# Two transformer layers on one Trainium2 core: PSUM banks by a plan of what is free first, the experts' weighted sums on GpSimd

## The chip, the cores and the metric

The program runs on one core of one Trainium2 chip. The metric is the device time of one execution in microseconds (us); the figure of a kernel is the median over its runs.

## The reference

Input x is 4 sequences of 1024 tokens of width 128, float32. Two layers follow, each of the form x + attention(norm(x)) + feed-forward(norm(x)), 16 heads of width 8.

```
layer 0: xn = layernorm(x)
         attention: q, k with rotary positions, softmax(q k^T / sqrt(8)) v, output matrix and bias (not causal)
         experts:   scores = xn @ gate_w + gate_b; the best 2 of 8 experts; softmax over the two scores
                    out = sum over the two: p_i * (relu(xn @ w1[e] + b1[e]) @ w2[e] + b2[e])
         x = x + attention + experts
layer 1: xn = layernorm(x)
         attention: causal, softmax(q k^T / sqrt(8)) v, output matrix
         ffn:       xq, w quantized blockwise (16) to FP4 and back; h = silu(xq @ wg) * (xq @ wu); quantized h @ wd
         x = x + attention + ffn
```

## The kernel before, in words

**Phases and slots.** A phase is one layer of one sequence (PHASES, eight of them, numbered 0 to 7: layer 0 of sequences 0 and 1, then layer 1 of sequence 0, and so on). The class Plan lays all work into 491 slots before the program is written. A slot holds one `step` (for four heads: scores with keys on the partitions, 128 keys by 512 queries, called E), one `quad` of a later set of rows (for four heads: scores with queries on the partitions, called M, of which only the row maxima are wanted), the `pv` product of the step before (into the PSUM tile pO), and side work: `xs` (PSUM-filling work such as projections, expert units `unit` and `y`, transposes), `small` (VectorE steps), `act`/`late` (ScalarE), `pool` (GpSimd) and `sp` (DMA issues). Each engine walks through the slots in order and executes its part; semaphores tie them.

**PSUM.** pO has one bank of its own. The other seven banks are the ring (RING = 7). Every E (one head), every M (one head) and every entry of `xs` takes one bank. TensorE writes E, `exps` on ScalarE (L854) reads it into PR; TensorE writes M, `maxima` on VectorE (L1201, and L1205 for masked tiles of layer 1) reduces it into mparts. In this kernel the n-th claim takes bank n mod 7, and before it `vacant` lets TensorE wait until the claim seven back has been read out (s_ex for E, s_mr for M, s_xA or s_xD for an entry of xs). TensorE executes in order: what waits holds up all that stands behind it.

```
r = plan.at[kind][k] - RING
if r >= 0:
    was, of = plan.ring[r]
```

**The experts' sum.** The tokens are scattered to rows in HBM ordered by expert (L784), 23 units of 128 rows go through the experts, and the results come back by indirect DMAs (`gather`, L800), eight tiles of 128x128 for the first expert (k = 0) into yg, which is the tile ra, and then eight for the second (k = 1). After each eight, VectorE's step `comb` adds them into the residual xr: 8 instructions of 128x128 (L1381), each xr = yg * weight + xr with the weight a number per partition, in four steps of two. So there are 4 sequences x 2 x 8 = 64 of them. The gathers of k = 1 wait on s_comb for the sums of k = 0, and the statistics of layer 1 (`stats`) come some slots behind the last sum. ra also serves as `sums` in the projections with rotary positions.

**GpSimd** has in its queue: the variance's power -1/2, the split of projections into bf16 parts (L759, L763, L767), scatters and gathers, and the rounding to FP4 (`round`, L811 to L831).

**VectorE and GpSimd lines** the text speaks of: L1268 normalises, L1381 is the experts' sum, L1439/L1440 split the row maxima for the tile msplit, L831 is a 128x512 product with an operand repeated along its blocks, L759 a 128x512 sum.

## Time and profile before

| what | value |
|---|---|
| median of 3 runs | 1598.43 us (1593.64 to 1598.57) |
| the profiled execution, its own time | 1606.22 us |
| its span | 1604.5 us |
| busy TensorE / VectorE / ScalarE / GpSimd | 91% / 83% / 70% / 36% of the span |
| mean granted TensorE clock | 0.956 of full speed |
| time per slot (491 slots) | 3.3 us |

PE in a row is TensorE, PEld its weight loads, DVE VectorE, ACT ScalarE, POOL GpSimd, SP SyncE, which issues most DMAs. A busy PE includes the modelled end of each matmul. "Lxxx" is a line of the kernel before.

### The profile page before, as it was taken

How to read it: one execution, taken by the hardware profiler on the slowest of the kernel's cores; microseconds unless marked ns; L12 is line 12 of the kernel's file. 1: busy time of each engine (PE TensorE's matmuls, PEld its weight loads, DVE VectorE, ACT ScalarE, POOL GpSimd, SP SyncE). 2: the span in 40 equal slices, each digit the busy share in tenths (PEclk: the TensorE clock that was granted, in tenths of full speed). 3: DMA queues.
4: the chain of work that ended last, by engine and by line, in shares of the span. 5: the costliest groups of instructions: out<-in, count | busy, mean ns of one | idle time of the engine just before them, and what ended most of it. 6: DMA issues, size and time to landing. Idle time of an engine off the chain costs nothing.

```text
span 1604.5 us, 34217 instructions
## 1 busy us (share of the span) xinstructions
PE 1459.2 (91%) x10557; PEld 583.9 (36%) x10557; DVE 1338.2 (83%) x3450; ACT 1129.7 (70%) x2580; POOL 578.4 (36%) x531
## 2 busy tenths in 40 slices
PE   3978989999999899989999999989999988989986
PEld 1112344443333544432333444333433432323332
DVE  6999877789887698999888789889878779978991
ACT  2267678788787467777878767768878845765675
POOL 3002302103253456440242263660152464554443
PEclk8599999999999899999999999999999977989998
DMA  6403273333271452221451135123372100600000
GB/s 172 102 8 100 73 184 110 106 87 91 88 183 52 120 116 83 59 82 36 134 120 51 37 113 134 49 82 99 111 165 82 39 26 2 152 9 15 2 2 14
DMA packets 169833, 131.84 MB, mean 82 GB/s; under 512 B 31597, under 2 KB 143158, under 8 KB 169654
## 3 DMA queue, kind: packets, MB, share of 16 engines
q1 hardware_dynamic: 165562, 121.26, 28.5%
q0 software_dynamic: 4096, 8.40, 1.7%
q8 instruction: 91, 1.49, 0.4%
q14 instruction: 84, 0.69, 0.1%
HBM read 88.50 MB, written 40.50 MB: 80 GB/s over the span
## 4 chain that ended last, share of the span: by engine, by line
PE 58%; DVE 26%; issue 6%; ACT 5%; POOL 3%; DMA 1%; SPq 0%; another core or an unknown queue 0%; DVEq 0%; ACTq 0%; POOLq 0%
PE ring L542 38%; PE pO L542 17%; DVE mparts L1201 15%; PE ring L545 3%; ACT PR L854 3%; DVE junk L1205 2%; DVE xr L1381 1%; DVE stats L1251 1%; ACT hid L925 1%; DVE hs L1493 1%; DVE xr L1501 1%; DVE am L1414 1%; DMA b1r<-in_b 1%; ACT parts L548 0%; DVE hs L1489 0%
## 5 line engine op out<-in xcount | busy, mean ns | idle before, releaser
L854 ACT ACTIVATE PR<-ring 128x512 f32<-128x512 f32 (+3 forms) x1792 | 882.4, 557 | 344.8 <-PE ring L542 333.7
L1201 DVE TENSOR_REDUCE mparts<-ring 128x1 f32<-128x512 f32 x1280 | 808.5, 682 | 84.4 <-PE ring L542 77.1
L542 PE MATMUL ring<-QX,KX 50*128 50x512 bf16 (+3 forms) x1792 | 543.7, 366 | 77.2 <-DVE mparts L1201 35.5
L542 PE MATMUL ring<-KX,QX 48*128 48x512 bf16 (+3 forms) x1792 | 556.8, 374 | 14.2 <-DMA QX<-scratch 14.1
L542 PE MATMUL pO<-PR,VX 128*18 128x512 f32 (+3 forms) x3584 | 444.0, 568 | 6.5 <-ACT PR L854 5.2
L542 PEld LDWEIGHTS ring<-QX,KX 50*128 50x128 bf16 x1792 | 127.5, 94 | 609.0 <-ACT PR L854 220.3
L1205 DVE CUSTOM_DVE_ANT_0 junk<-ring,diag 128x384 bf16<-128x384 f32 (+3 forms) x512 | 228.8, 486 | 46.0 <-PE ring L542 41.2
L811 POOL TENSOR_SCALAR bq<-bq 128x352 f32<-128x352 f32 (+1 forms) x40 | 47.2, 1179 | 349.7 <-ACT bq L964 349.3
L784 POOL DMA_INDIRECT rows_in<-xn,at x64 | 63.7, 996 | 228.8 <-PE pO L542 144.8
L542 PEld LDWEIGHTS ring<-KX,QX 48*128 48x128 bf16 x1792 | 127.3, 94 | 33.6 <-DVE mparts L1201 17.9
L925 ACT ACTIVATE hid<-ring,b1r 128x128 f32<-128x128 f32 x368 | 105.0, 369 | 27.7 <-PE ring L542 26.2
L542 PE MATMUL ring<-yx,w1r 128*128 128x128 f32 x736 | 107.8, 291 | 7.7 <-DMA b1r<-in_b 4.8
L542 PEld LDWEIGHTS pO<-PR,VX 128*18 128x18 f32 x3584 | 60.6, 96 | 132.0 <-issue 88.0
L800 POOL DMA_INDIRECT ra<-rows_out,at x64 | 61.6, 963 | 125.4 <-PE pO L542 89.2
L542 PEld LDWEIGHTS ring<-yx,w1r 128*128 128x128 f32 x736 | 91.7, 196 | 34.3 <-DVE mparts L1201 23.3
L542 PE MATMUL ring<-w2r,hid 128*128 128x128 f32 x736 | 97.5, 275 | 0.0
L542 PEld LDWEIGHTS ring<-w2r,hid 128*128 128x128 f32 x736 | 93.2, 197 | 0.9 <-issue 0.5
L767 POOL TENSOR_TENSOR parts<-rb,parts 128x512 bf16<-128x512 f32 x30 | 35.0, 1166 | 115.3 <-ACT parts L548 115.3
L542 PE MATMUL ring<-identb,laterb 128*128 128x128 bf16 x512 | 75.2, 230 | 0.0
L825 POOL TENSOR_SCALAR yq<-yq 128x352 f32<-128x352 f32 (+1 forms) x40 | 60.3, 1508 | 3.3
L820 POOL TENSOR_TENSOR bq<-hq,bq 128x352 f32<-128x352 f32 x64 | 59.7, 933 | 4.6
L548 ACT ACTIVATE yx<-ring 128x256 f32<-128x256 f32 (+1 forms) x96 | 36.0, 375 | 35.2 <-PE ring L542 33.8
(165 smaller groups left out, 1349.8 us busy)
## 6 DMA issues: line engine op xcount, KB each, us to landing
w1r<-in_w SPq DMA_DIRECT2D x92, 256.0 KB
w2r<-in_w SPq DMA_DIRECT2D x92, 256.0 KB
scratch<-parts SPq DMA_DIRECT2D x48, 256.0 KB, 3.3
scratch<-parts SPq DMA_DIRECT2D x96, 128.0 KB, 2.3
KX<-scratch SPq DMA_DIRECT2D x64, 192.0 KB, 4.4
QX<-scratch SPq DMA_DIRECT2D x128, 96.0 KB, 5.0
xg<-rows_in SPq DMA_DIRECT2D x92, 64.0 KB
rows_out<-yx SPq DMA_DIRECT2D x92, 64.0 KB
```

The costliest lines, as they stand in the source:

```text
L542: return nc.tensor.matmul(dst, lhsT, rhs, start=start, stop=stop, **kw)
L545: return nc.tensor.transpose(dst, src, ident[0:src.shape[0], 0:src.shape[0]])
L548: return nc.scalar.activation(dst, src, ACT.Copy)
L784: nc.gpsimd.indirect_dma_start(xs[b % 2], bass.IndirectOffsetOnAxis(at[b % 2][:, c:c + 1], 0), xn[0][:, c % T, :], None).then_inc(s_sc[b], 16)
L800: nc.gpsimd.indirect_dma_start(yg[:, D * t:D * t + D], None, ys[b % 2], bass.IndirectOffsetOnAxis(at[b % 2][:, c:c + 1], 0)).then_inc(s_yg ...
L811: ins = nc.gpsimd.tensor_scalar(b_, b_, 1.0, None, ALU.max)
L820: ins = nc.gpsimd.tensor_tensor(b_, dst, b_, ALU.subtract)
L825: ins = nc.gpsimd.tensor_scalar(y, y, SHIFT, SHIFT, ALU.add, ALU.subtract)
L854: nc.scalar.activation(PR[:, n % 2, HALF * j + off:HALF * j + HALF], ring[plan.bank("E", k)][:, off:HALF], ACT.Exp, scale=SCALE).then_inc( ...
L925: ins = nc.scalar.activation(hid[N % 2][:, P * fc:P * fc + P], src[:, P * fc:P * fc + P], ACT.Relu, bias=b1r[N % 2][:, fc:fc + 1])
L1201: v.tensor_reduce(dst, src[:, 0:w], axis=X, op=ALU.max).then_inc(s_mr, 1)
L1205: v.tensor_tensor_reduce(out=junk[k % 2][:, 0:w], in0=src[:, 0:w], in1=diag[:, HALF - w:HALF], scale=1.0, scalar=NEG, op0=ALU.add, op1=ALU ...
```

## The change

Two things change. First, Plan gets a method `banks`: it walks through all slots with a cost for each piece of work on TensorE, ScalarE and VectorE, keeps for each engine a clock in its own units, and gives each claim the bank that this account frees first. `vacant` then waits for whatever was last in that bank. Second, `comb` leaves VectorE's lists and goes to GpSimd's, with two halves of 512 columns instead of four steps of two tiles: a product of yg with the weights (128x512, weight repeated along a tile's columns) in place, then a sum into xr. GpSimd waits between the two on a new semaphore s_mul. s_comb now counts four per sequence, and VectorE waits on it before `stats` of layer 1, before `soft1`, and before each write of a projection (`pj`), since ra is shared. The steps after the sums of sequences 0 and 3 (phases 2 and 7: stats, projections, stores, loads) come one to three slots later.

```diff
@@ Plan
+    def banks(self):
+        work = {"P": [], "A": [], "D": []}
...
+        freeing = {"E": "ex", "M": "mx"}
+        time, at, clock, place = {}, [], {"P": 0, "A": 0, "D": 0}, {"P": 0, "A": 0, "D": 0}
+        held = [None] * RING
+        self.bank_of, self.was = {}, {}
+        def advance(who):
+            while place[who] < len(work[who]):
+                cost, needs, takes, gives = work[who][place[who]]
+                if any(t not in time for t in needs):
+                    return
+                clock[who] = max([clock[who]] + [time[t] + LAG for t in needs])
+                if takes is not None:
+                    free = lambda b: -1 if held[b] is None else time.get(held[b][1], math.inf)
+                    b = min(range(RING), key=free)
+                    clock[who] = max(clock[who], free(b) + LAG)
+                    self.bank_of[takes], self.was[takes] = b, held[b] and held[b][0]
...
     def bank(self, kind, k):
-        return self.at[kind][k] % RING
+        return self.bank_of[kind, k]
@@ tiles
-            i = self.chain("comb", i + T // 2 + 1, [("comb", p, k, h) for h in range(T // 2)], 2 if p in (1, 3) else 1)[-1] + 1
+            i += T // 2 + 1
+            for h in range(NH):
+                self.slot(i)["pool"].append(("comb", p, k, h))
+                i += 1
@@ gpsimd
-                                pool.wait_ge(s_comb, 2 * b + k)
+                                pool.wait_ge(s_comb, 4 * b + 2 * k)
...
+                        if e[0] == "comb":
+                            _, p, k, h = e
+                            b = PHASES[p][1]
+                            if h == 0:
+                                pool.wait_ge(s_yg[k], 16 * T * (b + 1))
+                                pool.wait_ge(s_xn, T * (p + 1))
+                            g_ = yg[:, HALF * h:HALF * h + HALF]
+                            g3 = g_.rearrange("p (t d) -> p t d", d=D)
+                            w3 = pr[b % 2][:, k, TH * h:TH * h + TH].rearrange("p (t o) -> p t o", o=1).to_broadcast([P, TH, D])
+                            nc.gpsimd.tensor_tensor(g3, g3, w3, ALU.mult).then_inc(s_mul, 1)
+                            pool.wait_ge(s_mul, 4 * b + 2 * k + h + 1)
+                            if k or h:
+                                pool.wait_ge(s_comb, 4 * b + 2 * k + h)
+                            pool.wait_ge(*freed(("fp", p, h)))
+                            dst = flat(xr[b % NX], h)
+                            nc.gpsimd.tensor_tensor(dst, dst, g_, ALU.add).then_inc(s_comb, 1)
@@ tensor
-                    r = plan.at[kind][k] - RING
-                    if r >= 0:
-                        was, of = plan.ring[r]
+                    if plan.was[kind, k] is not None:
+                        was, of = plan.was[kind, k]
@@ vector
+                        if layer and e[2] == 0:
+                            dve.wait_ge(s_comb, 4 * (b + 1))
...
+                        if b >= 2:
+                            dve.wait_ge(s_comb, 4 * (b - 1))
                         count(v.reciprocal(pr[b % 2][:, 0, :], ev1[:, :]))
...
-                    if kind == "comb":
...
-                            ins = v.scalar_tensor_tensor(xr[b % NX][:, t, :], yg[:, D * t:D * t + D], pr[b % 2][:, i, t:t + 1],
-                                                         xr[b % NX][:, t, :], ALU.mult, ALU.add)
...
+                            if added:
+                                dve.wait_ge(s_comb, added)
```

**TensorE, phase 1, layer 0 of sequence 1.** QX,KX is an E, KX,QX an M, w2r,hid the second product of an expert unit; the digit behind ring is the bank. Before:

```order
L542 MATMUL ring0<-QX1,KX1 128x512 [waits s_mr,s_ex]
L542 MATMUL ring1<-KX1,QX1 128x512
L542 MATMUL ring2<-QX1,KX1 128x512 [waits s_ex,s_xA]
L542 MATMUL ring3<-KX1,QX1 128x512
L545 MATMUL ring4<-ident,oT0 128x128 [waits s_oT,s_mr]
...
L542 MATMUL ring5<-w2r0,hid0 128x128 [waits s_xA,s_ex]
...
L542 MATMUL ring6<-QX1,KX1 128x512 [waits s_ex,s_mr]
L542 MATMUL ring0<-KX1,QX1 128x512
L542 MATMUL ring1<-QX1,KX1 128x512 [waits s_ex,s_mr]
```

The same place of the changed kernel:

```order
L636 MATMUL ring0<-QX1,KX1 128x512 [waits s_mr,s_ex]
L636 MATMUL ring3<-KX1,QX1 128x512
L636 MATMUL ring6<-QX1,KX1 128x512 [waits s_xA,s_mr]
L636 MATMUL ring4<-KX1,QX1 128x512
L639 MATMUL ring2<-ident,oT0 128x128 [waits s_oT,s_mr]
...
L636 MATMUL ring5<-w2r0,hid0 128x128 [waits s_xA,s_ex]
...
L636 MATMUL ring1<-QX1,KX1 128x512 [waits s_mr,s_ex]
L636 MATMUL ring3<-KX1,QX1 128x512
L636 MATMUL ring0<-QX1,KX1 128x512 [waits s_ex]
```

The work and its order are the same; the banks no longer go round, and the last pair shown waits for ScalarE's reading alone where it waited for both engines.

**VectorE, in phase 1, the first sums of sequence 0** (mparts is a row maximum). Before:

```order
L1201 TENSOR_REDUCE mparts<-ring 128x1 [waits s_m] x14
L1381 SCALAR_TENSOR_TENSOR xr<-ra,pr,xr 128x128 [waits s_dve,s_xn,s_yg0]
L1381 SCALAR_TENSOR_TENSOR xr<-ra,pr,xr 128x128
L1381 SCALAR_TENSOR_TENSOR xr<-ra,pr,xr 128x128 [waits s_dve]
L1381 SCALAR_TENSOR_TENSOR xr<-ra,pr,xr 128x128
L1201 TENSOR_REDUCE mparts<-ring 128x1 [waits s_m] x2
```

In the changed kernel one row, `L1312 TENSOR_REDUCE mparts<-ring 128x1`, with its wait on s_m and the count 28, stands there instead: the sums are gone and the maxima follow one another.

**GpSimd, the same place, changed kernel** (before, the gathers of k = 1 follow at once behind those of k = 0, their first with a wait on s_comb):

```order
L894 DMA ra<-rows_out,at 128x128 [waits s_mr]
L906 TENSOR_TENSOR ra<-ra,pr 128x512 [waits s_xn,s_yg0]
L914 TENSOR_TENSOR xr<-xr,ra 128x512 [waits s_xD,s_mul]
L906 TENSOR_TENSOR ra<-ra,pr 128x512
L914 TENSOR_TENSOR xr<-xr,ra 128x512 [waits s_xD,s_comb,s_mul]
L894 DMA ra<-rows_out,at 128x128 [waits s_comb,s_lo,s_pv]
```

Four 128x512 instructions now stand between the two sets of gathers, and the first of them waits until the gathered tiles have landed (s_yg0).

## Rows read from the trace of the kernel before

**Rows 1.** The page's parts 1 and 4: busy time per engine; the chain's shares by engine.

```profile
PE 1459.2 (91%) x10557; PEld 583.9 (36%) x10557; DVE 1338.2 (83%) x3450; ACT 1129.7 (70%) x2580; POOL 578.4 (36%) x531
...
PE 58%; DVE 26%; issue 6%; ACT 5%; POOL 3%; DMA 1%; SPq 0%; another core or an unknown queue 0%; DVEq 0%; ACTq 0%; POOLq 0%
```

**Rows 2.** The chain of waits, its shares by line.

```profile
by line: PE ring L542 37.6%; PE pO L542 17.1%; DVE mparts L1201 14.8%; issue 6.2%; PE ring L545 3.4%; ACT PR L854 3.1%; DVE junk L1205 1.6%; DVE xr L1381 1.1%; DVE stats L1251 0.8%; ACT hid L925 0.6%; DVE hs L1493 0.5%; DVE xr L1501 0.5%; D
```

**Rows 3.** Waits of PE: for whom, us in total, times, longest us.

```profile
PE ring L542 <- DVE mparts L1201: 45.3, 97, 2.1
PE ring L542 <- ACT PR L854: 23.0, 49, 2.1
...
PE ring L542 <- DVE mparts L1205: 6.6, 10, 2.5
PE ring L545 <- DVE mparts L1201: 5.5, 11, 1.1
```

**Rows 4.** Waits of DVE, same columns.

```profile
DVE mparts L1201 <- PE ring L542: 77.1, 172, 5.0
DVE junk L1205 <- PE ring L542: 41.2, 67, 2.3
```

**Rows 5.** Stretches: length, busy us of PE, PEld, DVE, ACT, POOL (count), PEclk, DMA.

```profile
330.00:350.00 20.00, 20.00 (x156) 8.70 (x152) 16.41 (x29) 17.14 (x41) 0.00 (x0) 1.00 0.35 99
100.00:160.00 60.00, 50.76 (x367) 11.85 (x365) 57.98 (x117) 46.74 (x91) 15.63 (x16) 1.00 0.25 71
```

**Rows 6.** Groups by line: count, then busy us and mean ns, idle before.

```profile
L854 ACT ACTIVATE PR<-ring 128x512 f32<-128x512 f32 (+3 forms) x1792 | 882.4, 557 | 344.8 <-PE ring L542 333.7 <-PE pO L542 3.5 <-issue 2.1
L1201 DVE TENSOR_REDUCE mparts<-ring 128x1 f32<-128x512 f32 x1280 | 808.5, 682 | 84.4 <-PE ring L542 77.1 <-issue 1.1
...
L1381 DVE SCALAR_TENSOR_TENSOR xr<-ra,pr,xr 128x128 f32<-128x128 f32 x64 | 24.3, 420 | 0.3
```

**Rows 7.** Stretches around L1381 in eight places, last two and the sum of all.

```profile
1296.00:1300.00 4.00, 1.45 (x10) 0.75 (x11) 3.96 (x11) 1.16 (x3) 3.07 (x3) 0.86 0.00 0
1323.00:1330.00 7.00, 5.03 (x26) 1.29 (x27) 6.86 (x17) 3.43 (x7) 5.80 (x6) 0.73 0.05 12
sum 55.00, PE 45.62 PEld 18.59 DVE 54.41 ACT 39.57 POOL 23.23; mean PE 5.70 PEld 2.32 DVE 6.80 ACT 4.95 POOL 2.90
```

**Rows 8.** Tiles xr, ra, xn, msplit: duration ns min/median/max, first and last start.

```profile
L1381 DVE SCALAR_TENSOR_TENSOR xr<-ra,pr,xr x64: 334/346/1083, 375.1 to 1328.3; 128x128 f32<-128x128 f32 x64
...
L759 POOL TENSOR_TENSOR ra<-ra,rb x12: 1263/1272/1278, 179.8 to 946.5; 128x512 f32<-128x512 f32 x12
...
L831 POOL TENSOR_TENSOR xn<-yq,sc x8: 1056/1058/1088, 447.8 to 1433.8; 128x512 f32<-128x512 f32 x8
...
L1440 DVE TENSOR_TENSOR msplit<-mneg,msplit x64: 174/175/878, 57.5 to 1564.7; 128x16 bf16<-128x16 f32 x64
```

**Rows 9.** Timeline of DVE (start, us, instruction), then a stretch behind it as in Rows 5.

```profile
1296.85 2.53 DVE L1381 SCALAR_TENSOR_TENSOR xr<-ra,pr,xr 128x128 f32<-128x128 f32 x4
...
1300.26 1.25 DVE L1381 SCALAR_TENSOR_TENSOR xr<-ra,pr,xr 128x128 f32<-128x128 f32 x4
...
1300.00:1315.00 15.00, 15.00 (x72) 6.15 (x73) 9.80 (x31) 3.93 (x10) 3.88 (x4) 0.50 0.07 19
```

**Rows 10.** First loads of phase 2 (SP queue), their landing, first masked maximum of phase 2.

```profile
456.69 0.34 SPq L647 DMA_DIRECT2D KX<-scratch  x1
...
DMA to landing us min/median/max: 3.0/4.3/6.1
...
475.60 0.29 DVE L1205 CUSTOM_DVE_ANT_0 junk<-ring,diag 128x128 bf16<-128x128 f32 x1
```

More of the change, by code:

```diff
@@ L40 @@
          "xq": 9, "hq": 6}
+ON_TENSOR = {"unit": 13, "y": 14, "turn": 8, "xT": 11, "v": 13, "cT": 11, "xqT": 11, "of": 11, "wT": 10, "pj": 17,
+             "mtr": 4.6, "fin": 11, "gu": 12.5, "down": 9, "fp": 18, "lg": 13, "rt": 8}
+EMPTIES = {"unit": 16.5, "y": 6.2, "turn": 7, "xT": 8, "v": 9, "cT": 8, "xqT": 8, "of": 8, "wT": 8, "pj": 10, "mtr": 4,
+           "fin": 12.5, "gu": 8.7, "down": 5, "fp": 11.5, "lg": 4, "rt": 5}
+STEP = {"stats": 6.6, "means": 4.4, "norm": 8.4, "best": 2.8, "which": 4.5, "hits": 4.5, "comb": 8.8, "rem": 10, "wq": 18}
+SIDE, PV, MASK, LAG = 3.7, 13.5, 4, 4.5
 class Plan:
@@ L99, in __init__ @@
         self.number()
+        self.banks()
     def kts(self, p, qh):
@@ L488, in two_layer_block @@
         s_comb = sem("s_comb")
+        s_mul = sem("s_mul")
         s_th, s_yq, s_ab, s_rd, s_pl = sem("s_th"), sem("s_yq"), sem("s_ab"), sem("s_rd"), sem("s_pl")
@@ L1339, in small_step @@
                         if b >= 2:
-                            dve.wait_ge(s_comb, 2 * (b - 1))
+                            dve.wait_ge(s_comb, 4 * (b - 1))
                         count(v.tensor_copy(at[b % 2][:, :], posf[:, :]))
@@ L1372, in small_step @@
                         v.tensor_tensor(cw[b % 2][:, :, 0:E], w4[:, 0], w4[:, 1], ALU.add).then_inc(s_cw, 1)
-                    if kind == "comb":
-                        _, p, i, h = e
-                        b = PHASES[p][1]
-                        if h == 0:
-                            dve.wait_ge(s_yg[i], 16 * T * (b + 1))
-                            dve.wait_ge(s_xn, T * (p + 1))
-                        own()
-                        for t in (2 * h, 2 * h + 1):
-                            ins = v.scalar_tensor_tensor(xr[b % NX][:, t, :], yg[:, D * t:D * t + D], pr[b % 2][:, i, t:t + 1],
-                                                         xr[b % NX][:, t, :], ALU.mult, ALU.add)
-                            if t == T - 1:
-                                ins.then_inc(s_comb, 1)
-                                dve.wait_ge(s_comb, 2 * b + i + 1)
-                            else:
-                                count(ins)
                     if kind == "rem":
@@ L1427, in small_step @@
                                                    wide(ri, width), ALU.mult, ALU.mult).then_inc(s_yq, 1)
+                added = 0
                 for s in plan.slots:
@@ L1508, in _ @@
                         small_step(e)
+                    added += len([e for e in s["pool"] if e[0] == "comb"])
         nc.all_engine_barrier()
```

56 lines of the change are left out of this document (added).

## The prediction

> **What bounds the kernel now.** I read the page first. TensorE is busy 91% of the span and VectorE 83%, and the chain that ended last runs 58% through TensorE and 26% through VectorE [rows 1]: no engine bounds it alone. By line, the products into the ring and into pO hold most of it, and the row maxima L1201 are next with 14.8%; the experts' sums L1381, a small line, hold 1.1%, 17.6 us of the 1604.5 [rows 2]. Two stretches show the two regimes. From 330 to 350 us TensorE is busy in all 20 us and VectorE has 16.4: there no bank and no VectorE work matters. From 100 to 160 us VectorE is busy 58.0 of 60 us and TensorE 50.8: TensorE waits for banks, but VectorE has no time left to drain them sooner [rows 5]. The change can earn where neither holds. The waits of TensorE's products for a bank of the ring, all four rows together, are 45.3 + 23.0 + 6.6 + 5.5 = 80.4 us [rows 3]. In turn VectorE's maxima wait 77.1 + 41.2 us for TensorE [rows 4]. Both engines wait for each other at different times, which a looser coupling can shrink.
>
> The profiled execution took 1606.2 us, 7.8 above the median of 1598.4; the sum is made against 1606.2 and 7.8 is taken off at the end. Of the difference between two kernels of this length, about 0.3% (4.8 us) can be told from nothing.
>
> **Part 1: 64 sums leave VectorE.** They are 64 x 420 ns = 24.3 us busy [rows 6]. In the eight stretches that hold them, 55 us long, VectorE is busy 54.4 us and TensorE 45.6 [rows 7]: VectorE bounds there and TensorE idles 9.4 us. When the sums go, TensorE can win its idle time and then bounds itself, so I take 9.4. The ends are 0 (the next wait takes it over) and 24.3.
>
> **Part 2: 32 instructions on GpSimd.** Each half is a product with a repeated operand and a sum; the nearest rows of 128x512 are L831 (1.06 us, one operand repeated) and L759 (1.27 us) [rows 8]. So 16 x (1.06 + 1.27) = 37 us, at most 41 with 1.27 for both, on an engine busy 36% [rows 1]. They stand in the queue with the gathers, the rounding and the bf16 parts, and the first waits there until the gathers have landed, which holds up a rounding for a few us; the rounded tiles have slots of cover, so I price it 0. A pair of halves takes 2 x 2.33 = 4.7 us. Who waits next is VectorE at `stats` of layer 1, three or four slots (10 us or more at 3.3 us a slot) behind: covered. If that cover were gone, the last pair would cost 4.7 us in each of 4 sequences, 19 us. Phases 2 and 7 get their loads one to three slots later. In phase 2 the first load was issued at 456.7 us, landings took 4.3 us, and the phase's first masked maximum began at 475.6 [rows 10]: 14.6 us are spare, and three slots are 10. Price 0; if the store in front comes late too, up to 5 us are lost. SyncE's queue is only reordered by these loads.
>
> The added waits of VectorE (before each pj, `soft1`, `stats`) are for sums whole slots back; behind a late one the maxima would queue, and TensorE would wait for their banks. I price them at 0 with that same cover.
>
> VectorE and GpSimd disturb each other in this trace. The tiny L1440, two operands from SBUF, takes 174 ns at the least, 175 in the median and 878 at the most, and L1381 runs 334, 346 and 1083 [rows 8]; the mean of L1381 lies 74 ns above its median, 4.7 us in total. At 1296.85 us four of them took 2.53 us where four others took 1.25 [rows 9], with GpSimd busy 3.07 of those 4 us [rows 7]. The removed lines are among those that suffer; the new GpSimd work meets mostly maxima that read PSUM. I set the balance at 0, from -5 to +24 (32 instructions each stretching one VectorE instruction by 1083 - 334 ns). The Trainium skill (SBUF — State Buffer, Who interferes with whom) says that a VectorE instruction with two SBUF inputs and a GpSimd instruction that reads SBUF exclude each other for the whole instruction; by that the kernel before suffers on L1381, which the trace bears out, and the change swaps the sides.
>
> **Part 3: the banks.** The order of the work stays, only the claim waited for changes. I counted both plans: 4135 claims; before, each waits for the claim seven back. Now 1467 still do, 1340 get a bank claimed 8 to 12 back, an older product and so likelier read out, and 1321 one claimed 2 to 6 back, where the account expects the older ones to be held longer. Its costs fit the trace: in its units a 512-column exponential is 7.8 and a maximum 10, against 557 and 682 ns [rows 6], a ratio of 1.28 against 1.22. Without the 9.4 us of part 1, 80.4 - 9.4 = 71 us of bank waits are left. About a third of the claims got an older bank, which would be 24 us; some of the nearer claims will bite, and some waits belong to stretches in which VectorE is full. I take 18. The ends: all 71 gained, or the loss of rival D.
>
> **Part 4: the clock.** After the pause at 1296 to 1300 us, in which TensorE was busy 1.45 of 4 us [rows 7], the granted clock is 0.50, the 1.2 GHz level, from 1300 to 1315 with TensorE busy all 15 us [rows 9]. At 2.4 GHz that work would take half, 7.5 us less. That pause came from the sums, which are gone. I take 5, since VectorE and the masked tiles may cause another; ends 0 and 15 (a second such stretch follows at 0.73 [rows 7]).
>
> **Sum:** 9.4 + 18 + 5 = 32.4; 1606.2 - 32.4 = 1573.8; less 7.8 gives **1566.0 us**, 2% faster.
>
> **The rivals.**
>
> *B, the banks bring nothing* (chance 0.20). The waits move, since both engines are nearly full; parts 1 and 4 stay: 1598.4 - 14.4 = 1584. For it: in rows 5 no stretch of either regime has anything to win. Against it: VectorE's 118 us of waits [rows 4].
>
> *C, the work runs smoothly* (chance 0.12). Most bank waits go and with them pauses before which the clock fell: 17.6 for the sums, 40 of the 71, 8 for the clock, 1598.4 - 65.6 = 1533. For it: the chain's 26% in VectorE. The Trainium skill (TensorE: Matmul & The Clock Gate, A second HAM failure mode: psum-queue depth-cycling) describes short idle times between groups of matmuls that cycle through PSUM banks and a clock that then goes up and down; it points to this rival.
>
> *D, the fixed plan waits where the round would not have* (chance 0.13, slower). Place: `vacant` before the ring's products. Where the account is wrong by one drain, TensorE waits for a bank that is not free while another is. I counted the claims that must wait until at most one later product of the same kind is outstanding: 339 now, 66 before. A wait for the maxima lasts 45.3 / 97 = 0.47 us on average [rows 3]. If 92 of the 273 more bite, 43 us are lost against 14.4 gained: 1627. It decides from 14.4 / 0.47 = 31 of them.
>
> *E, the sums cost on GpSimd what they gave* (chance 0.10). The change then does not unload VectorE: each of the 32 holds a VectorE instruction by 0.75 us, 24 us off the forecast's gain: 1590. The largest excesses in rows 8 are for it, that the medians lie at the minima is against it. By the skill's rule in part 2, with a whole L759 as the hold, it would be 41 us and not 24, 1607.
>
> **How the numbers follow.** The forecast A has 0.45, and its time is the prediction. Faster by over 0.3% (below 1593.6) are A, C, nearly all of B and 0.06 of E: 0.45 + 0.12 + 0.16 + 0.06 = 0.79. Slower (above 1603.2) is D, 0.13; the rest, 0.08, lies within. The range reaches from C's time to a little above no change, 1533 to 1602: it leaves out most of D, half of C and little else.
>
> **What would show each step.** Right: L1381's place is taken by 32 GpSimd instructions of 1.06 to 1.3 us; VectorE's busy time falls by some 24 us; TensorE's ring waits for maxima and exponentials fall from 80 to about 55 us, VectorE's for TensorE too; no clock at 0.50 right behind the sums of sequence 3. TensorE's busy time may fall a little, since each break leaves the modelled end of a matmul. Wrong: a new wait of `stats`, pj or GpSimd's rounding on s_comb; ring waits at 80 us or more (B or D); GpSimd's new instructions at 2 us or VectorE's small ones at twice their medians (E); PE idle at the start of phase 2 behind QX or KX loads.

## Result and profile after

The changed kernel is slower by 0.4%, not faster by 2%: its median is 1604.47 us over 20 runs, that of the kernel before 1598.44 us over 20 runs on the same chip; the ratio is 1.0036, 95% interval 1.0019 to 1.0053. One of the 20 runs took 1779.7 us and has no weight in the comparison. The profiled execution took 1601.92 us, with a span of 1599.8 us and a mean granted clock of 0.944, against 0.956 before.

The page's first part of the kernel after (against [rows 1]), then TensorE's waits (against [rows 3]) and VectorE's (against [rows 4]): for whom, us in total, times, longest. L636 is the product into ring or pO that was L542, L639 the transpose that was L545, L966 the exponential that was L854, L1312 and L1316 the maxima that were L1201 and L1205, L943 the last step of rounding that was L831.

```profile
PE 1455.0 (91%) x10557; PEld 580.2 (36%) x10557; DVE 1318.4 (82%) x3386; ACT 1132.0 (71%) x2580; POOL 614.6 (38%) x563
```

```profile
PE ring L636 <- ACT PR L966: 35.4, 69, 1.2
PE ring L636 <- DVE mparts L1312: 23.0, 51, 2.2
...
PE ring L639 <- POOL hq L943: 9.5, 3, 3.8
PE ring L636 <- DVE mparts L1316: 7.0, 12, 2.1
...
PE ring L639 <- POOL xn L943: 4.0, 3, 1.8
...
PE ring L639 <- DVE mparts L1312: 1.4, 2, 1.2
...
DVE mparts L1312 <- PE ring L636: 102.4, 210, 5.1
DVE junk L1316 <- PE ring L636: 39.2, 60, 2.1
...
DVE sc L1520 <- POOL hq L943: 8.5, 4, 3.8
```

Three things are to be seen. TensorE's bank waits for VectorE fell from 45.3 + 6.6 + 5.5 = 57.4 to 23.0 + 7.0 + 1.4 = 31.4 us, but those for ScalarE rose from 23.0 to 35.4, so that 66.8 of 80.4 us are left. New are waits for GpSimd's rounding: 9.5 us of TensorE, 8.5 of VectorE. And VectorE, 20 us less busy, waits 102.4 us for TensorE where it waited 77.1: its spare time was not used.

The new instructions have the durations that were expected. Tiles ra, xr and msplit: duration min/median/max in ns, first and last start (against [rows 8]).

```profile
L906 POOL TENSOR_TENSOR ra<-ra,pr x16: 1029/1038/1040, 381.1 to 1330.5; 128x512 f32<-128x512 f32 x16
L914 POOL TENSOR_TENSOR xr<-xr,ra x16: 1260/1273/1513, 382.2 to 1331.6; 128x512 f32<-128x512 f32 x16
...
L1541 DVE TENSOR_TENSOR msplit<-mneg,msplit x64: 174/175/879, 56.5 to 1560.0; 128x16 bf16<-128x16 f32 x64
```

**Where the time goes.** Two profiled executions differ by chance too, so I laid out for each kernel when the first exponential of each slot starts, and compared the time that each stretch of slots took. Slots 38 to 54 took 55.7 us before and 69.4 after, 13.7 more; from there on the kernel after gained back. (A stretch of slots a to b runs from the first exponential of slot a to that of slot b.) These slots as a whole, before and then after, columns as in [rows 5]:

```profile
65.20:120.90 55.70, 45.38 (x284) 11.62 (x283) 53.52 (x129) 35.30 (x69) 4.14 (x4) 0.86 0.10 28
...
64.20:133.70 69.50, 56.12 (x285) 14.06 (x283) 54.78 (x129) 36.77 (x70) 4.14 (x4) 0.67 0.08 23
```

For the same work TensorE is busy 10.7 us longer at a mean granted clock of 0.67 instead of 0.86; its waits for banks of the ring grew by 3.4 us alone, from 9.7 to 13.1. The middle of this place in stretches of 10 us, first of the kernel before:

```profile
76.00:86.00 10.00, 7.18 (x42) 1.75 (x41) 9.69 (x28) 4.83 (x9) 0.00 (x0) 0.83 0.00 0
86.00:96.00 10.00, 8.29 (x50) 1.87 (x51) 9.41 (x34) 5.38 (x12) 0.00 (x0) 0.83 0.02 4
96.00:106.00 10.00, 8.80 (x64) 2.77 (x63) 9.86 (x24) 8.09 (x18) 0.00 (x0) 1.00 0.03 7
```

The same stretches of the kernel after, then rows of its timeline (start, us, instruction, idle before it and who ended that):

```profile
76.00:86.00 10.00, 7.70 (x33) 3.41 (x33) 6.42 (x18) 2.88 (x5) 0.00 (x0) 0.50 0.00 0
86.00:96.00 10.00, 7.04 (x29) 0.97 (x27) 7.74 (x30) 3.58 (x6) 0.00 (x0) 0.50 0.00 1
96.00:106.00 10.00, 8.26 (x42) 2.15 (x42) 6.53 (x18) 5.43 (x11) 0.00 (x0) 0.66 0.01 3
```

```profile
85.61 0.60 PE L636 MATMUL ring<-QX,KX 50*128 50x512 bf16 x1 [0.72 <-ACT PR L966]
85.62 0.60 PE L636 MATMUL ring<-KX,QX 48*128 48x512 bf16 x1
...
89.44 0.58 PE L636 MATMUL ring<-QX,KX 50*128 50x512 bf16 x1 [0.84 <-ACT PR L966]
89.45 0.61 PE L636 MATMUL ring<-KX,QX 48*128 48x512 bf16 x1
90.71 0.29 PE L636 MATMUL ring<-identb,msplit 128*32 128x128 bf16 x1 [0.66 <-ACT PR L966]
```

TensorE issues a pair of products, then waits 0.7 to 0.8 us for the exponential of that pair: the plan gave the next product a bank that was claimed only just before. In three stretches it issues 104 instructions where it issued 156, VectorE runs dry (6.42 of 10 us busy against 9.69), and the granted clock stays at 0.50, the 1.2 GHz level, until 102.9 us; before, it stood at 0.83 and then 1.00. Whether the waits hold the clock down or the low clock makes the waits, these rows don't say.

### The profile page after: what moved, and what is told of

The parts are those of the page before. It is cut to its first block and busy times, and to the rows that moved or that the text cites. A ratio compares the mean times of both kernels' runs of the same rounds, so it can differ in the third digit from the quotient of the medians.

```text
span 1599.8 us, 34215 instructions
## 1 busy us (share of the span) xinstructions
PE 1455.0 (91%) x10557; PEld 580.2 (36%) x10557; DVE 1318.4 (82%) x3386; ACT 1132.0 (71%) x2580; POOL 614.6 (38%) x563
## 5 line engine op out<-in xcount | busy, mean ns | idle before, releaser
L966 ACT ACTIVATE PR<-ring 128x512 f32<-128x512 f32 (+3 forms) x1792 | 882.3, 557 | 338.0 <-PE ring L636 331.5
L1312 DVE TENSOR_REDUCE mparts<-ring 128x1 f32<-128x512 f32 x1280 | 808.6, 681 | 108.2 <-PE ring L636 102.4
L636 PE MATMUL ring<-QX,KX 50*128 50x512 bf16 (+3 forms) x1792 | 542.2, 369 | 73.2 <-ACT PR L966 31.2
L636 PE MATMUL ring<-KX,QX 48*128 48x512 bf16 (+3 forms) x1792 | 553.0, 377 | 13.9 <-DMA QX<-scratch 13.8
L636 PE MATMUL pO<-PR,VX 128*18 128x512 f32 (+3 forms) x3584 | 450.0, 575 | 8.0 <-ACT PR L966 6.8
L636 PEld LDWEIGHTS ring<-QX,KX 50*128 50x128 bf16 x1792 | 124.2, 94 | 598.6 <-issue 175.8
L1316 DVE CUSTOM_DVE_ANT_0 junk<-ring,diag 128x384 bf16<-128x384 f32 (+3 forms) x512 | 228.0, 486 | 42.5 <-PE ring L636 39.2
L636 PEld LDWEIGHTS ring<-KX,QX 48*128 48x128 bf16 x1792 | 124.1, 94 | 33.3 <-DVE mparts L1312 17.9
L1037 ACT ACTIVATE hid<-ring,b1r 128x128 f32<-128x128 f32 x368 | 105.0, 369 | 25.7 <-PE ring L636 24.3
L636 PE MATMUL ring<-yx,w1r 128*128 128x128 f32 x736 | 107.7, 291 | 7.0 <-DMA b1r<-in_b 5.2
L636 PEld LDWEIGHTS pO<-PR,VX 128*18 128x18 f32 x3584 | 60.8, 97 | 135.1 <-issue 91.8
L636 PEld LDWEIGHTS ring<-yx,w1r 128*128 128x128 f32 x736 | 91.7, 196 | 32.4 <-ACT PR L966 17.5
L636 PE MATMUL ring<-w2r,hid 128*128 128x128 f32 x736 | 98.4, 277 | 0.1
L636 PEld LDWEIGHTS ring<-w2r,hid 128*128 128x128 f32 x736 | 94.1, 199 | 1.2 <-DVE mparts L1316 0.4
L636 PE MATMUL ring<-identb,laterb 128*128 128x128 bf16 x512 | 74.9, 229 | 0.0
L937 POOL TENSOR_SCALAR yq<-yq 128x352 f32<-128x352 f32 (+1 forms) x40 | 60.3, 1507 | 3.3
L934 POOL TENSOR_SCALAR yq<-yq 128x352 f32<-128x352 f32 (+1 forms) x40 | 60.2, 1504 | 0.2
```

The source lines that it names most:

```text
L636: return nc.tensor.matmul(dst, lhsT, rhs, start=start, stop=stop, **kw)
L934: ins = nc.gpsimd.tensor_scalar(y, y, -1.0, 1.0, ALU.max, ALU.min)
L937: ins = nc.gpsimd.tensor_scalar(y, y, SHIFT, SHIFT, ALU.add, ALU.subtract)
L966: nc.scalar.activation(PR[:, n % 2, HALF * j + off:HALF * j + HALF], ring[plan.bank("E", k)][:, off:HALF], ACT.Exp, scale=SCALE).then_inc( ...
L1037: ins = nc.scalar.activation(hid[N % 2][:, P * fc:P * fc + P], src[:, P * fc:P * fc + P], ACT.Relu, bias=b1r[N % 2][:, fc:fc + 1])
L1312: v.tensor_reduce(dst, src[:, 0:w], axis=X, op=ALU.max).then_inc(s_mr, 1)
```

## The experiments

There are 18 runs in five groups (e1 to e4, e5 to e8, e9 to e12, e13 to e16, e17 and e18); each group has its own letters for the theories. Every kernel is compared with the kernel before, run beside it on the same chip (medians of that kernel: 1608.0, 1597.1, 1607.3, 1597.7 and 1607.1 us in the five groups). The results first, as a table of three switches: the banks, where the sums are made, and whether the steps behind the sums of sequences 0 and 3 stand at their old slots.

| banks | sums on VectorE, old slots | sums on GpSimd, old slots | sums on GpSimd, two slots later |
|---|---|---|---|
| rotation | 1 (before) | 0.9997 (e12) | 1.0048 (e2) |
| full plan | 0.9980 (e1) | 0.9972 (e14) | 1.0036 and 1.0051 (the change; e4) |
| plan, rotation up to slot 62 | 0.9940 (e5) | 0.9910 (e8) | 0.9981 (e7) |
| plan, last five banks closed | 0.9889 and 0.9878 (e6, e15) | 0.9901 and 0.9867 (e9, e16) | 0.9963 (e11) |

Rotation, sums on VectorE and two slots later is 1.0055 (e13). The half width of the intervals is 0.0017 to 0.0036. Times of single stretches of slots come from one profiled execution of each kernel; e9 and e16, which are one and the same kernel, take 32.0 and 35.8 us in slots 134 to 142, so a difference of 4 us in one stretch of one pair can be chance.

### One part alone

**e1_banks** is the kernel before with the method `banks`:

```diff
     def bank(self, kind, k):
-        return self.at[kind][k] % RING
+        return self.bank_of[kind, k]
...
-                    r = plan.at[kind][k] - RING
-                    if r >= 0:
-                        was, of = plan.ring[r]
+                    if plan.was[kind, k] is not None:
+                        was, of = plan.was[kind, k]
```

> The bank plan alone; the experts' sums stay on VectorE as before. Theory Q (GpSimd's queue: the sums there hold up the rounding to FP4, the plan itself helps): the trace of the changed kernel shows 67.7 us of ring waits where 80.4 stood, so about 10 us are gained, 1585 to 1593, ratio 0.992 to 0.997. Theory P (the fixed plan gives nothing, waits only change sides and the clock takes back the rest): within 0.4% of before, 1594 to 1606.

Measured: 1606.14 us, ratio 0.998 (0.9962 to 0.9999). In slots 38 to 54 it loses 7.7 us, in 134 to 142 4.1 and in 358 to 374 5.4; elsewhere it gains. The last of these is no loss of the plan: e1, e5, e14 and the change claim the same banks in slots 354 to 374, and take 68.4, 62.1, 66.2 and 61.3 us there, against 63.0 before. Its waits from 66 to 122 us:

```profile
PE ring L631 <- ACT PR L943: 11.3, 18, 0.8
PE ring L631 <- DVE mparts L1289: 0.6, 1, 0.6
```

and those of the kernel before from 66 to 120 us:

```profile
PE ring L542 <- DVE mparts L1201: 8.9, 13, 2.1
PE ring L542 <- ACT PR L854: 0.4, 1, 0.4
```

The wait for VectorE was exchanged for one on ScalarE that is about as long. So the plan is worth 3 us, not 18, and something in it gives back what it earns.

**e2_sums** is the changed kernel with the banks in rotation:

```diff
     def bank(self, kind, k):
-        return self.bank_of[kind, k]
+        return self.at[kind][k] % RING
```

> The sums on GpSimd alone; the banks go round as before. Theory Q: the turns wait for the rounding as in the changed kernel (three waits of up to 3.8 us, about 9 us), the clock falls behind them, 1603 to 1615, ratio 1.003 to 1.010. Theory P: the sums bring what leaving VectorE is worth, 5 to 10 us, 1588 to 1594.

Measured: 1614.73 us, ratio 1.0048 (1.0023 to 1.0072). The half of the change that was to give 14 us loses 7. That lies in the range of theory Q, but GpSimd's queue is not the whole cause, as e12 and e13 show below.

**e3_behind** is the changed kernel, but in a slot that has a rounding and a sum the rounding goes first:

```diff
-            s["pool"].sort(key=lambda e: e[0] in ("scatter", "gather"))
+            s["pool"].sort(key=lambda e: 2 if e[0] in ("scatter", "gather") else e[0] == "comb")
```

> The changed kernel, but in a slot that has a rounding step and a sum the rounding goes first. Theory Q: the 3.8 us waits of TensorE for the rounded tile shrink to under 2 us, and the kernel gains 5 us or more on the changed one, near 1598 or below. Theory P: no difference that can be told from the changed kernel, 1601 to 1608, since the next wait takes over.

Measured: 1612.23 us, ratio 1.0026 (1.0005 to 1.0047); TensorE's waits for the rounded hq are 5.6 us. **e4_same** is the change again on this chip:

> The changed kernel again on the same chip as the three above, so that they can be compared with it. Both theories: ratio to before 1.002 to 1.006, mean clock 0.940 to 0.950 where before has about 0.95.

Measured: 1614.69 us, ratio 1.0051 (1.0026 to 1.0075), with 7.2 us of those waits. By the medians the queue's order is worth a quarter of a per cent, and the intervals overlap; neither theory's 5 us shows. It doesn't explain e2.

### The banks: what the plan gives back

**e5_round**: the first 263 claims (up to slot 62) in rotation, sums on VectorE.

```diff
-                    b = min(range(RING), key=free)
+                    n = self.at[takes[0]][takes[1]]
+                    b = n % RING if n < 263 else min(range(RING), key=free)
```

> The kernel before with the plan of banks, but its first 263 claims (up to slot 62) take the banks in rotation, as before; the sums stay on VectorE. Theory S: the plan has a loss in one place (slots 38 to 54, where kernels with it came 8 to 14 us later than kernels without, at a granted clock of 0.50) and earns some 10 us after it. Then slot 54 is reached within 2 us of the kernel before, the gain of the later slots stays, and the time falls by 8 to 16 us: ratio 0.990 to 0.995, mean granted clock 0.951 or more. Theory N: a fixed plan earns nothing lasting, and what it loses at one place it would lose at another: ratio 0.996 to 1.002, as for the full plan.

Measured: 1587.15 us, ratio 0.994 (0.9917 to 0.9963), clock 0.956. Slot 54 is reached 0.5 us behind the kernel before. Slots 134 to 142 still lose 4.2.

**e6_far**: from the first slot, but none of the five banks claimed last may be given.

```diff
-        held = [None] * RING
+        held, recent = [None] * RING, []
...
-                    b = min(range(RING), key=free)
+                    b = min([b for b in range(RING) if b not in recent], key=free)
+                    recent.append(b)
+                    del recent[:-5]
```

> The kernel before with the plan of banks from the first slot, but no claim may take one of the five banks claimed last, so each takes the one of the two others that the plan has free first; claims on a bank with at most one later product of its kind fall from 350 to 183 (66 in the kernel before). Theory S: what costs is the short distance, so the start's loss is halved or gone and the time is 0.990 to 0.996 of before; ScalarE's ring waits fall from 41.6 us towards the 23 us of before. Theory N: the gain comes from free choice alone, a choice of two gives nothing: 0.998 to 1.003.

Measured: 1579.62 us, ratio 0.9889 (0.9869 to 0.991). Run again as **e15_far_again**:

> The kernel before with the plan of banks closed to the five banks claimed last, a second time and on the same chip as the next: 0.987 to 0.991, as the first time (0.9889).

Measured: 1579.54 us, ratio 0.9878 (0.9855 to 0.9901). Against the kernel before it takes 0.7 us less in slots 38 to 54, 0.2 less in 134 to 142, and 2.5 (e6) and 3.4 (e15) less in 358 to 374. The gain is larger than either theory had it. TensorE's waits of e15 in full:

```profile
PE ring L633 <- DVE mparts L1291: 26.2, 65, 2.1
PE ring L633 <- ACT PR L945: 22.5, 57, 2.2
```

Those for the maxima fell from 45.3 to 26.2 us and those for ScalarE stayed at the 23 of before. The full plan has 16 (e1) and 23 (the change) for the maxima, but 42 and 35 for ScalarE. A choice between two banks holds the whole gain; the choice among seven moves waits from one engine to the other. e5 and e6 differ by 0.5%, so keeping the start in rotation gives back less than half of what the closed banks give; where the rest is gained I can't name.

**e10_far4**: the same with four banks closed (`del recent[:-4]`).

> The kernel before with the plan of banks, closed to the four banks claimed last instead of five, sums on VectorE. Claims on a bank with at most one later product of its kind: 287, against 183 with five and 350 with none. If the short distance is what costs, the time lies between these two, 0.991 to 0.996, and slot 54 is reached 1 to 6 us later than in the kernel before. If any small restriction heals it, 0.988 to 0.990.

Measured: 1592.28 us, ratio 0.9899 (0.9863 to 0.9935), slot 54 reached 4.4 us late. The time falls in the range of the rival ("any small restriction heals it"), and its interval reaches over both; only the place is as the distance has it: the loss in slots 38 to 54 against before goes 7.7, 4.3 and -0.7 us with none, four and five banks closed.

Why did the plan choose those banks? Its account has one speed for TensorE. **e17_halfclock** doubles TensorE's costs up to slot 80, with no bank closed:

```diff
                 cost, needs, takes, gives = work[who][place[who]]
+                cost *= 2 if who == 'P' and place['P'] < 480 else 1
```

> The kernel before with the full plan of banks (no bank closed), in whose account TensorE's costs are doubled up to slot 80; sums on VectorE. In this account 7 claims of slots 32 to 63 fall on a bank with at most one later product of its kind, against 40. Theory C (the plan loses at the start because its account has TensorE at full speed where the granted clock is half): slot 54 is reached within 2 us of the kernel before, and the time is 0.989 to 0.995. Theory F (any bank given out freely there costs): slot 54 is still 5 us or more late, and the time is 0.996 to 1.000.

Measured: 1595.89 us, ratio 0.9937 (0.9915 to 0.996); slots 38 to 54 take 0.7 us less than before. The free choice is harmless there once the account has a speed nearer to the one that the clock grants; by the plans, 7 claims of slots 32 to 63 then have at most one later product outstanding, not 40. Slots 134 to 142, where the factor has ended, take 4.1 us more than before, as in e1. **e18_slowpe** has a factor of 1.5 everywhere:

> The same with TensorE's costs times 1.5 in the whole account: 174 such claims against 350. Theory C: an account that is pessimistic on TensorE gives up little and loses nothing at slots 38 to 54, 134 to 142 and 358 to 374, so 0.986 to 0.991, like the plan that is closed to the five banks claimed last (0.989 and 0.988). Theory F: the fixed distance is what heals, not the account, and this is 0.993 or more.

Measured: 1600.73 us, ratio 0.9966 (0.9946 to 0.9985). The three places of e1 now stand at +2.7, -0.7 and -0.7 us against before, but the gain is gone too. The waits of e18:

```profile
PE ring L632 <- DVE mparts L1290: 42.2, 89, 1.7
PE ring L632 <- ACT PR L944: 16.7, 37, 1.7
```

The 0.986 to 0.991 of theory C is missed. With TensorE held for slow everywhere, the choice is no better than the rotation: the waits for the maxima are back near the 45 us of before. So the loss of slots 38 to 54 comes from the account's speed for TensorE and the near banks that it gives out for it (e17; e5, e6 and e10 take the near banks away by other means). For the other two places that isn't shown. One other factor for all stretches doesn't mend the plan; closing the newest banks does.

**How large that loss is goes with the clock.** e1, e3, e4, e14 and the change claim the same banks up to slot 54, and do the same work there. In e1 the granted clock came up to 1.00 at 71.4 us, fell again at 81.7, and 7.7 us were lost. In the other four it stayed at 0.50 until 102.9 to 108.6 us, and 13.1 to 15.6 us were lost.

### The sums, and the two slots

**e7_both**: the changed kernel with its first 263 claims in rotation (the edit of e5).

> The kernel after the change with its first 263 claims in rotation: its banks as in the run with rotation at the start, the sums on GpSimd. Theory S with GpSimd's queue: it stands 3 to 8 us above the run with rotation at the start and sums on VectorE (the queue at slots 222 to 230 costs 3 to 5 us, the later preparation in slots 406 to 414 another 5 to 7 us, against 4 to 6 us gained where the sums stood), so 0.993 to 0.999 of before. Theory N: 1.002 to 1.005, like the change itself.

Measured: 1594.68 us, ratio 0.9981 (0.9959 to 1.0003). **e8_unshift** adds one edit, so that the steps behind the sums of sequences 0 and 3 stand where they stood. The text ahead of the prediction calls them phases 2 and 7, one to three slots later. Laid side by side, the two plans show more: the preparation of phase 3 follows that of phase 2 through the same slots, and 118 of its pieces move too, most by two to four slots and 15 to an earlier one; the feed-forward of phase 2 moves by up to six slots. All of it, phase 3 included, is what e8 puts back:

```diff
-        self.done[p] = max(self.done.get(p, 0), i + 1)
+        self.done[p] = max(self.done.get(p, 0), i + (1 if p in (1, 3) else -1))
```

> The run before this one, with the steps behind the sums of sequences 0 and 3 (phases 2 and 7: statistics, projections, stores, loads) at the slots that they have in the kernel before, two earlier. If the later preparation costs the 5 to 7 us seen in slots 406 to 414, this is 3 to 7 us faster than the run before it, and slots 406 to 414 take what they take in the kernel before. If that loss has another cause (the sums' place in GpSimd's queue, the clock), it stays, and the two are within 2 us; VectorE's wait for the sums ahead of the statistics would then cost up to 3 us more.

Measured: 1583.22 us, ratio 0.991 (0.9891 to 0.993). It is 11.5 us faster than e7, more than the 3 to 7 expected. Slots 406 to 414 take 27.4 us, as before (27.7), where e7 takes 32.4.

**e13_late** turns this round: the kernel before, nothing changed but that the same steps come later again (`i + (1 if p in (1, 3) else 3)`).

> The kernel before (rotation, sums on VectorE) with one edit: the steps behind the sums of sequences 0 and 3 come two slots later, as in the change. Theory L (the later preparation itself collides with the other side work): ratio 1.002 to 1.006, with 4 us or more lost in slots 406 to 414 or 446 to 454. Theory Q (it is the sums in GpSimd's queue together with it): within 0.2% of before.

Measured: 1607.59 us, ratio 1.0055 (1.0034 to 1.0075). The delay alone (two slots in phase 7, one to six in phases 2 and 3, within a slot or two of the change's), with the old banks and the old sums, costs 9 us. **e14_plan_gp** is the change with the edit of e8:

> The changed kernel with one edit: the steps behind the sums of sequences 0 and 3 at the slots of the kernel before; banks by the plan with no restriction. The change measured 1.0036 and 1.0051. Theory L: the later preparation costs some 0.5% at any plan, so 0.997 to 1.001. Theory Q: it stays at 1.002 to 1.005.

Measured: 1595.74 us, ratio 0.9972 (0.9949 to 0.9995), against the 1.0036 and 1.0051 of the change. **e11_far_late** is the change with five banks closed, the delay kept, and **e9_far_gp** the same without the delay:

> The changed kernel with one edit alone: no claim may take one of the five banks claimed last; the preparation of phases 2 and 7 stays two slots later. If the later preparation costs 5 to 10 us at any plan (11 us of the clock's and the chip's scatter included, it did so with rotation at the start): 0.992 to 0.996, and slots 406 to 414 take 5 us more than in the kernel before. If that loss comes of the short distance, this is within 0.2% of the first of these four.

> The changed kernel with two edits: no claim may take one of the five banks claimed last, and the steps behind the sums of sequences 0 and 3 stand at the slots that they have in the kernel before. Theory K (GpSimd's sums are worth 2 to 5 us once they move nothing else): 2 to 5 us below the same plan with sums on VectorE, which measured 0.989, so 0.985 to 0.988. Theory Q (the sums hold up the rounding and give nothing, whatever the plan): 0.989 to 0.992.

Measured on one chip: e11 1600.48 us, ratio 0.9963 (0.9942 to 0.9985), just above the 0.992 to 0.996 expected; e9 1590.59 us, ratio 0.9901 (0.9865 to 0.9937). Over five pairs (e13, e2 over e12, the change over e14, e7 over e8, e11 over e9) the delay costs 0.5 to 0.8%.

Where? The stretches of slots agree over the pairs: slots 174 to 182 take 1.1 to 4.3 us more, 206 to 214 1.6 to 3.0, 222 to 230 1.4 to 7.0, 406 to 414 5.0 to 7.2 more, while 158 to 174 take 4 to 7 less and 398 to 406 take 0.6 to 5.6 less. Together that is -0.1, 3.7, 8.1, 12.6 and 4.0 us in the five pairs, where the ratios say 8 to 12: part of the cost is not placed. (The profiled execution of e13 is also the fastest of its runs.) One place in full, of e13: VectorE's queue with GpSimd's beside it, TensorE behind it, then stretches of it.

```profile
1348.44 2.33 DVE L1268 TENSOR_SCALAR xn<-xr,mv,rstd 128x128 f32<-128x128 f32 x4 [0.56 <-POOL rstd L752]
1350.69 0.41 DVE L1205 CUSTOM_DVE_ANT_0 junk<-ring,diag 128x256 bf16<-128x256 f32 x1
...
1348.39 0.92 POOL L828 TENSOR_TENSOR yq<-yq,bq 128x352 f32<-128x352 f32 x1
1349.39 0.78 POOL L831 TENSOR_TENSOR hq<-yq,sc 128x352 f32<-128x352 f32 x1
...
1351.17 0.60 PE L542 MATMUL ring<-QX,KX 50*128 50x512 bf16 x1 [1.99 <-DVE mparts L1205]
```

```profile
1345.00:1350.00 5.00, 3.18 (x33) 1.05 (x32) 4.39 (x14) 2.54 (x7) 3.19 (x3) 0.83 0.00 0
1350.00:1355.00 5.00, 2.69 (x10) 1.03 (x10) 4.97 (x17) 1.79 (x4) 0.17 (x1) 0.50 0.00 0
1355.00:1360.00 5.00, 4.94 (x30) 1.55 (x34) 4.06 (x15) 2.65 (x5) 0.00 (x0) 0.64 0.01 2
```

The normalising steps of phase 7 now stand where TensorE's work changes from narrow masked tiles to full ones. VectorE waits for rstd, then works 2.33 us on four tiles while the masked maxima queue behind, and TensorE waits 1.99 us for their bank. Two of the four tiles take 955 and 936 ns where the median of this kernel is 340: each begins within 0.07 us of one of GpSimd's two rounding steps and ends within 0.09 us of its end. So 1.2 of the 2.33 us go with GpSimd's steps beside them. TensorE is busy 2.69 of 5 us, and the granted clock is 0.50 as the full tiles begin. Slots 406 to 408 take 11.9 us in e13 and 6.9 before. Ahead of that, in 402 to 404, it is the kernel before that has the collision (10.7 us against 7.9), but with narrow tiles. That the delay costs is shown; of its 9 us only this place is traced to an instruction, and which of the moved steps costs the rest stays open.

**e12_gp_round** has the sums on GpSimd, old slots and rotation: part 1 and part 2 of the prediction with nothing else.

> The kernel before with its banks in rotation throughout and the sums on GpSimd, the steps behind the sums of sequences 0 and 3 at their old slots. The sums with their later preparation measured 1.0048. Theory K: without the later preparation they gain: 0.996 to 0.999. Theory Q: the queue's delays at slots 206 to 230 (3 to 5 us) remain and outweigh the gain at slots 390 to 406: 1.000 to 1.004.

Measured: 1607.31 us, ratio 0.9997 (0.9979 to 1.0016): nothing. Beside the better plan, on one chip with e15, **e16_far_gp_again**:

> The same plan with the sums on GpSimd and nothing moved, a second time. Theory K (the sums off VectorE are worth 2 to 5 us): 0.002 to 0.003 below the one before it. Theory Q (they give nothing): within 0.2% of it, as the two first runs were (0.9901 and 0.9889).

Measured: 1577.32 us, ratio 0.9867 (0.9839 to 0.9894), against 0.9878 of e15. The five pairs with the sums on the one or the other engine (e12, e14 to e1, e8 to e5, e9 to e6, e16 to e15) are -0.03, -0.08, -0.30, +0.12 and -0.11%: a gain of 1 us, less than can be told.

Where did the 9.4 us of part 1 go? They were won and given back at once. In the five pairs slots 392 to 394, the first sums of sequence 3, take 1.8 to 5.8 us less with the sums on GpSimd, and 394 to 396 take 1.5 to 4.7 more; slots 398 to 400, its second sums, take 2.2 to 3.3 less, and 400 to 402 take 3.8 to 5.6 more.

The kernel after shows what takes it back at the first of the two. GpSimd's queue, VectorE's and TensorE's, then the stretch behind:

```profile
1299.20 1.03 POOL L906 TENSOR_TENSOR ra<-ra,pr 128x512 f32<-128x512 f32 x1
1300.31 1.26 POOL L914 TENSOR_TENSOR xr<-xr,ra 128x512 f32<-128x512 f32 x1
1301.53 0.92 POOL L940 TENSOR_TENSOR yq<-yq,bq 128x352 f32<-128x352 f32 x1
1302.53 0.79 POOL L943 TENSOR_TENSOR hq<-yq,sc 128x352 f32<-128x352 f32 x1
1303.28 1.04 POOL L906 TENSOR_TENSOR ra<-ra,pr 128x512 f32<-128x512 f32 x1
...
1303.42 0.92 DVE L1520 TENSOR_SCALAR sc<-am 128x22 f32<-128x22 f32 x1 [3.85 <-POOL hq L943]
1304.27 0.68 DVE L1316 CUSTOM_DVE_ANT_0 junk<-ring,diag 128x512 bf16<-128x512 f32 x1
...
1305.71 0.58 PE L636 MATMUL ring<-QX,KX 50*128 50x512 bf16 x1 [2.06 <-DVE mparts L1316]
...
1305.00:1310.00 5.00, 3.04 (x17) 1.04 (x21) 4.77 (x12) 1.21 (x3) 1.87 (x2) 0.50 0.00 0
```

A product and a sum, 2.3 us, stand ahead of the last two steps of a rounding. VectorE's next scale (L1520) writes the tile sc, which L943 has yet to read, and waits 3.85 us; then the next product holds it: L1520 takes 0.92 us where the median is 178 ns. Behind it stands a masked maximum, and TensorE waits 2.06 us for its bank. That is the pause of [rows 7] again, in the same place and by another way, and the clock falls to 0.50 behind it as it did before [rows 9].

## Why the prediction was wrong

The forecast was a gain of 32.4 us, the measurement a loss of 6. By terms of the sum: part 1 had 9.4 and gave 0.5 (e12); parts 3 and 4 had 23 and gave 3 (e1); the delay of part 2 had 0 and cost 9 (e13).

**Part 2, "Phases 2 and 7 get their loads one to three slots later ... Price 0": the step that made it a loss.** It costs 0.55% or 9 us alone (e13), and turned a gain of some 0.3% (e14) into the loss. I priced the delay by the loads; no wait of TensorE for them grew enough to matter (in all 14.8 us for QX after, 14.1 before). But with the loads move statistics, normalising, projections and rounding, on engines that execute in order, and not those of phases 2 and 7 alone: the preparation of phase 3 moved too, which I had overlooked. What counts is beside which tiles they come to stand; that is traced in one place only.

**Part 3, 18 us for the banks.** The plan as written gave 0.2%, 3 us (e1): of the terms of the sum this one was furthest off. That such a plan can earn 18 us was right, though by luck, since the 18 was a share of the claims with an older bank and not worked out from any wait: with five banks closed the plan gives 1.1 to 1.2%, 17.5 and 18.2 us (e6, e15). The step that failed was "Its costs fit the trace", as shown for slots 38 to 54 by e17. I compared ScalarE's and VectorE's costs and never TensorE's with the granted clock, which the same rows show at 0.50 for long stretches [rows 9]. In the change TensorE's ring waits fell by 26.0 us for VectorE and rose by 12.4 for ScalarE, 13.6 in balance; the profiled execution has a mean clock of 0.944 where it was 0.956, and the median time is no shorter. That the clock took the 13.6 us back fits, but is argued.

**Rival D** named the mechanism: a fixed plan that gives out a bank with at most one later product outstanding. Such waits there are (40 of these claims stand in slots 32 to 63, none in the kernel before), but its price, 0.47 us for each of 92, was wrong: the loss is no sum over such claims. e6 still has 183 of them and gains 1.1%, and with the same 40 claims e1 loses 7.7 us in slots 38 to 54 where the change loses 13.7. The loss there was mostly time at 0.50, not time in waits.

**Part 1, 9.4 us.** VectorE's busy time fell by 19.8 us, near the 24.3 (64 x 420 ns is 26.9; 24.3 is the busy time, in which overlaps count once). The gain came at the sums' own slots of sequence 3 and was gone two slots behind, taken over by the next wait: the 0 end of my range. The sign I had named for "wrong", a new wait for GpSimd's rounding, is there with 9.5 and 8.5 us.

**Part 2, durations and contention.** 1038 and 1273 ns against the 1.06 and 1.27 us taken, GpSimd's busy time 36.2 us up against 37: right. "The rounded tiles have slots of cover, so I price it 0" was wrong, with waits of up to 3.8 us for the rounded hq (9.5 us of TensorE and 8.5 of VectorE in all). Contention stayed near the 0 taken: the maxima L1312 last 681 ns (682 before), L1541 175 in the median and 879 at most as before. **Rival E** is right in its sum, the sums gave back on GpSimd what they won, but hardly in its mechanism. It had each of the 32 hold a VectorE instruction by 0.75 us. Two did: L1520 takes 924 and 925 ns where its median is 178, at 1303.42 and 1330.64 us, each time begun 0.14 us behind the start of a product L906 and ended within 0.03 us of its end (the first is in the rows above). That is 1.5 us, not 24; the waits behind the queue are the larger part. So the exclusion for a whole instruction that the Trainium skill (SBUF — State Buffer, Who interferes with whom) describes does show in this trace, and on instructions with one tile read from SBUF, where I had applied it to those with two.

**Part 4, 5 us from the clock.** The clock went the other way, from 0.956 to 0.944, since the pause behind the sums stayed and slots 38 to 54 got a new one. The Trainium skill (TensorE: Matmul & The Clock Gate, A second HAM failure mode: psum-queue depth-cycling) describes short idle times between groups of matmuls that cycle through banks and a clock that goes up and down. I had used it for rival C; the trace agrees in part, and against the change: 0.66 to 0.84 us idle between pairs, but the granted clock does not go up and down there, it stays at 0.50.

**The sum of the parts as measured:** -0.20% (e1), -0.03% (e12), +0.55% (e13), together +0.32%; the change measured +0.36%. The parts add up, as far as intervals of 0.2% on each can tell.

## What to carry to other kernels

When a change shifts a chain of steps by a slot or two, first list from both plans every piece that moves (here a whole further phase did), then price the shift by what each moved step comes to stand in front of on its in-order engine, and beside on GpSimd; slack of the transfers says nothing about it, and one kernel with the shift alone settles it. A static plan of buffers should be wrong in a harmless direction: keep it from giving out the newest ones, and let it choose between the few oldest. That version, with sums on VectorE or GpSimd alike, is 1.0 to 1.3% faster than the kernel before (e6, e9, e15, e16).

## What was unexpected of the hardware

The time of one and the same program goes with its mean granted clock. Over 19 runs of the changed kernel the correlation is -0.96, and a clock lower by 0.01 goes with 11 us more; in the other kernels, most with fewer runs, that 0.01 goes with 5 to 14 us. So part of the difference between two runs of a kernel is how long TensorE stands at the 1.2 GHz level. A gain need not come that way: e6 and e15 have a median clock of 0.9555, the kernel before beside them 0.956 and 0.955. Profiled executions mislead here: that of e13 is the fastest of its 8 runs (1598.2 us, clock 0.960; the medians are 1607.6 and 0.9515).

One and the same piece of program can run at either level for tens of microseconds. The five kernels with the same banks up to slot 54 do, as told above: 1.00 from 71.4 us in one, from 102.9 to 108.6 in the others. In the change TensorE is busy 7.0 to 8.3 of 10 us meanwhile, half as fast while it works, and waits in between for a reader that it has just supplied. It looks as if the low level and the waits kept each other up; no run separates the two. In other places programs repeat themselves to a few tenths of a microsecond: slots 224 to 226 take 5.1 to 5.5 us in the kernels without the delay and 6.4 to 6.5 in all those that have the delay and the sums on GpSimd.
